# Prologue of an attention kernel by input tile and token half, maxima by query tile, queries one group ahead

## The reference

```python
sa, ca, ga, sb, cb, gb = silu(c) @ wmod            # six rows of 512, from one row c of 512
h = layernorm(x) * (1 + ca) + sa
q = rmsnorm(h @ wq_a.T) @ wq_b.T                   # 128 wide, then 32 heads of 64 + 64
ckv, k_pe = split(h @ wkv_a.T, [32, 64])
k_nope, v = split(rmsnorm(ckv) @ wkv_b.T, [64, 128])   # for each of 32 heads
q_pe, k_pe = rope(q_pe), rope(k_pe)
attn = softmax(causal(q_full @ k_full.T * scale))
x = x + floor(ga) * ((attn @ v) @ wo.T)
h = layernorm(x) * (1 + cb) + sb
x = x + floor(gb) * ffn(h)                         # silu(gate) * up, down, width 1376
```

## Time and profile before

| what | us |
|---|---|
| median of 3 runs (lowest, highest) | 862.09 (860.8, 863.05) |
| the profiled execution, its time | 862.18 |
| its span, first to last instruction | 860.4 |
| busy: PE, PEld | 785.7, 531.4 |
| busy: DVE, ACT, POOL | 533.1, 271.5, 327.7 |
| first scores of the eight groups | 140.49, 202.09, 262.66, 324.03, 384.58, 445.05, 505.65, 560.01 |
| last values of the eighth group, end of its last record | 610.16 |
| mean granted clock of PE (1 is full speed) | 0.958 |

### The profile page before, as it was taken

One profiled execution on the slowest core, in us unless ns is written; L12 is line 12 of the kernel. 1 busy time (PEld: TensorE's weight loads), 2 busy tenths in 40 slices (PEclk: granted clock), 3 DMA queues, 4 the chain that ended last, 5 costly groups with the idle time before them and its releaser, 6 DMA issues.

```text
span 860.4 us, 10667 instructions
## 1 busy us (share of the span) xinstructions
PE 785.7 (91%) x3968; PEld 531.4 (62%) x3968; DVE 533.1 (62%) x836; ACT 271.5 (32%) x402; POOL 327.7 (38%) x199
## 2 busy tenths in 40 slices
PE   5659597999998999999999999999799899999997
PEld 5658254564664655656656655544487688886886
DVE  3354484896896896987978977756465333222342
ACT  2360002333433433433343333343344332221220
POOL 9220022374574574484564663524344100000111
PEclk9895687999999999999999999999899899999999
DMA  8300714306107007016034057046000032220011
GB/s 343 114 0 1 158 52 98 64 1 131 32 0 161 2 2 161 1 32 132 1 70 93 1 106 262 2 147 220 1 1 0 1 111 74 73 65 1 24 38 37
DMA packets 30275, 60.49 MB, mean 70 GB/s; under 512 B 4656, under 2 KB 16688, under 8 KB 28432
## 3 DMA queue, kind: packets, MB, share of 16 engines
q1 hardware_dynamic: 29024, 57.11, 24.8%
q10 hardware_dynamic: 1200, 2.69, 0.8%
HBM read 32.40 MB, written 2.10 MB: 40 GB/s over the span
## 4 chain that ended last, share of the span: by engine, by line
PE 60%; issue 12%; DVE 8%; POOL 7%; SPq 4%; DMA 4%; ACT 3%; POOLq 0%; ACTq 0%; DVEq 0%
PE PS L691 14%; PE PS L585 7%; PE PS L530 6%; PE PS L662 5%; PE PS L588 5%; PE PS L586 5%; PE PS L601 4%; POOL PR L1389 3%; DMA Q<-TQ 3%; SPq L386 2%; PE PS L459 2%; PE PS L521 2%; PE PS L534 1%; POOL RE L1354 1%; PE PS L512 1%
## 5 line engine op out<-in xcount | busy, mean ns | idle before, releaser
L817 ACT ACTIVATE PR<-PS 128x1024 f32<-128x1024 f32 (+1 forms) x144 | 132.9, 929 | 262.1 <-PE PS L588 183.5
L1085 DVE TENSOR_REDUCE NMa<-PS 128x1 f32<-128x512 f32 (+3 forms) x216 | 140.3, 665 | 44.4 <-PE PS L534 29.0
L530 PE MATMUL PS<-KH,Q 96*128 96x512 f32 (+3 forms) x384 | 132.2, 400 | 12.7 <-DMA Q<-TQ 10.6
L585 PE MATMUL PS<-Q,KH 128*128 128x512 f32 x288 | 132.5, 460 | 3.7 <-DMA Q<-NM 2.6
L1389 POOL TENSOR_TENSOR PR<-PR 128x1024 f32<-128x1024 f32 (+3 forms) x56 | 119.8, 2139 | 27.9 <-ACT PR L817 24.1
L691 PE MATMUL PS<-Q 128*128 128x512 f32 (+1 forms) x528 | 123.2, 396 | 5.1 <-DVE Q L1253 4.5
L691 PEld LDWEIGHTS PS<-Q 128*128 128x128 f32 (+1 forms) x528 | 99.3, 189 | 28.1 <-DVE Q L1253 4.7
L588 PE MATMUL PS<-Q,KH 128*128 128x512 f32 x288 | 114.6, 398 | 0.0
L586 PE MATMUL PS<-Q,KL 128*128 128x512 f32 x288 | 114.3, 397 | 0.0
L530 PEld LDWEIGHTS PS<-KH,Q 96*128 96x128 f32 x384 | 71.9, 196 | 49.2 <-issue 20.1
L585 PEld LDWEIGHTS PS<-Q,KH 128*128 128x128 f32 x288 | 56.1, 195 | 60.1 <-issue 28.2
(11 more groups left out here) (161 smaller groups left out, 1084.4 us busy)
## 6 DMA issues: line engine op xcount, KB each, us to landing
Q<-TQ SPq DMA_DIRECT2D x96, 256.0 KB, 5.0
PR<-in_wmod SPq DMA_DIRECT2D x6, 1024.0 KB, 7.2
RT<-in_wo SPq DMA_DIRECT2D x4, 1024.0 KB, 4.9
TQ<-in_wo SPq DMA_DIRECT2D x4, 1024.0 KB, 4.9
WI<-in_gate_w SPq DMA_DIRECT2D x10, 256.0 KB, 3.2
WI<-in_up_w SPq DMA_DIRECT2D x10, 256.0 KB, 3.6
DI<-in_down_w SPq DMA_DIRECT2D x10, 256.0 KB, 3.6
TQ<-in_x ACTq DMA_DIRECT2D x2, 1024.0 KB, 10.3
```

The lines of the kernel that those rows point to most:

```text
L530: ins = pe.matmul(bank[:, i * w:(i + 1) * w], M.Q[0:KR, g % 2, 0, h0 + i, qt * P:(qt + 1) * P], M.KH[0:KR, lo:lo + w], start=(i == 0), sto ...
L585: pe.matmul(dst, M.KH[:, ks], M.Q[:, w % 2, 0, :, qs], start=True, stop=False)
L817: act.activation(tiles, banks, ACT.Exp).then_inc(S_.p, 1)
L1085: dve.tensor_reduce(dst, PS[:, bank_of(turn), 0:n * w].rearrange("p (h k) -> p h k", k=w), axis=AX.X, op=ALU.max, negate=True).then_inc(S_ ...
```

## The change

**Prologue.** The inputs arrive by tile, into a place of their own. Moments, root and reciprocal are taken by tile: those of tiles 0 to 2 ahead, the later ones inside the tile loop, three tiles ahead. hH and hL have four places each in place of two. The rotated key parts and the copy to V move from VectorE to GpSimd (`keys`), the two roots of a tile become one. The latents use one PSUM bank in place of two. Group 0's weight folds stand in the loop after tile 3, the queries of the first 512 tokens after tile 7, those of the second half behind the loop. Only group 0's queries are made in the prologue. The columns n = 2 and 3 of the modulation and the two gate rows move into the windows of groups 0 and 1, and their tables are loaded later and to other places. The zeros in rows 96 to 127 of KH, KL and Q go, and the score products read 97 or 96 rows.

**Maxima.** `PARTS` is sorted by token half first: 11 parts for query tiles 0 to 3, then 27 for tiles 4 to 7. Each half has its own 16 columns, transposition and transfer. The transposition of the first half of group w + 1 stands at the end of window w, that of the second half behind the values of step 1 of window w + 1; the scores wait for the first at step 0 and for the second at step 4. In the prologue only the first half of group 0 is made.

**Queries.** The window of group w holds the queries of group w + 1, at places 0.03 to 0.30, and its maxima from 0.36 on, which run over into window w + 1. A half is sent as four transfers of 384 KB, one for each head, as soon as it is ready. An add counts in the table with 560 columns a microsecond in place of 850.

```diff
-    return sorted(parts, key=lambda part: part[3] + part[4])
+    return sorted(parts, key=lambda part: (part[0] >= NS // 2, part[3] + part[4]))
 
 
 PARTS = maxima_parts()
+FIRST = sum(part[0] < NS // 2 for part in PARTS)
...
-        self.Q = take("Q", [P, 2, 2, HG, S], F32R)
+        self.Q = take("Q", [P, 2, 2, NQB, HG, QB], F32R)
-        self.NMa = take("NMa", [P, HG, NS])
+        self.NMa = take("NMa", [P, 2, HG, NS // 2])
-        self.NM = take("NM", [HG * NS, P], F32R)
+        self.NM = take("NM", [HG * NS // 2, 2, P], F32R)
-        self.hH = take("hH", [P, 2, KD, P], F32R)
-        self.hL = take("hL", [P, 2, KD, P], F32R)
+        self.x = take("x_in", [P, NS, D])
+        self.hH = take("hH", [P, 4, KD, P], F32R)
+        self.hL = take("hL", [P, 4, KD, P], F32R)
...
+        self.wmod = [self.PR[:, 0], self.PR[:, 1], late_mod[2], late_mod[0], late_mod[0], late_mod[1]]
...
-QUERY_PLACES = [(0.13, ("w", 0), 0.5), (0.14, ("w", 1), 0.15), (0.15, ("w", 2), 0.15), (0.25, ("even", 0), 1.2),
-                (0.28, ("odd", 0), 1.2), (0.36, ("lat", 0), 1.3), (0.40, ("split", 0), 0.0),
-                (0.54, ("even", 1), 1.2), (0.57, ("odd", 1), 1.2), (0.65, ("lat", 1), 1.3), (0.75, ("split", 1), 0.0)]
-WINDOW_US = 56.0
+QUERY_PLACES = [(0.03, ("w", 0), 0.5), (0.035, ("w", 1), 0.15), (0.04, ("w", 2), 0.15), (0.06, ("even", 0), 1.2),
+                (0.09, ("odd", 0), 1.2), (0.13, ("lat", 0), 1.3), (0.16, ("split", 0), 0.0),
+                (0.20, ("even", 1), 1.2), (0.23, ("odd", 1), 1.2), (0.27, ("lat", 1), 1.3), (0.30, ("split", 1), 0.0)]
+WINDOW_US = 60.0
...
+def maxima_places(parts, begin, end):
+
+    cost = [0.14 + PARTS[k][2] * PARTS[k][4] / 960 for k in parts]
     places = []
+    for n, k in enumerate(parts):
+        places.append((begin + (end - begin) * sum(cost[:n]) / sum(cost), ("part", k), cost[n]))
+        if k == FIRST - 1:
+            places.append((places[-1][0] + 0.015, ("rows", 0), 0.3))
+    return places + [(end + 0.01, ("join",), 0.1), (end + 0.02, ("rows", 1), 0.3)]
+
+
+
+FIRST_HALF = [[("part", w, k) for k in range(FIRST)] + [("rows", w, 0)] for w in range(G)] + [[]]
+SECOND_HALF = [[("part", w, k) for k in range(FIRST, len(PARTS))] + [("join", w), ("rows", w, 1)] for w in range(G)]
...
+    if w < G - 1:
+        coming = maxima_places(range(len(PARTS)), 0.36, 1.16)
+        places += [(place, (name[0], w + 1) + name[1:], busy) for place, name, busy in coming]
+        places += [(place, (name[0], w + 1) + name[1:], busy) for place, name, busy in QUERY_PLACES]
+    if w == 0:
+        rest = maxima_places(range(FIRST, len(PARTS)), 0.0, 0.22)
+        places += [(place, (name[0], w) + name[1:], busy) for place, name, busy in rest]
+        places += [(0.45, ("modrow", w, 0), 0.7), (0.60, ("modrow", w, 1), 0.7), (0.75, ("mod", w, 2), 0.2)]
+    else:
+                places += [(0.09, ("den", w - 1, 1), 0.7), (0.10, ("inv", w - 1, 1), 0.8), (0.17, ("norm", w - 1, 1), 0.0)]
+    if w == 1:
...
+            due = {("v", 1): SECOND_HALF[w], "last": FIRST_HALF[w + 1]}.get(spot, [])
+            while places and (any(name in due for _, name, _ in places) or max(places[0][0], free - SLACK) <= place):
...
+FIRST_FOLDS = [("w", 0, i) for i in range(3)]
+FIRST_QUERIES = [[(kind, 0, hf) for kind in ("even", "odd", "lat", "split")] for hf in range(2)]
+FIRST_MAXIMA = [("part", 0, k) for k in range(FIRST)] + [("rows", 0, 0)]
+BANKED = ("w", "even", "odd", "lat", "part", "rows", "den", "fold", "mod", "modrow")
...
-    def send_queries(g):
-        sp.wait_ge(S_.tl, 2 * (g + 1))
+    def send_queries(g, hf):
+        cols = slice(hf * 512, hf * 512 + 512)
+        sp.wait_ge(S_.tl, 2 * g + hf + 1)
         if g > 1:
             sp.wait_ge(S_.sc, NEXP * (g - 1))
         for h in range(HG):
-            for b in range(3):
-                sp.dma_start(M.Q[b * 32:(b + 1) * 32, g % 2, :, h, :].bitcast(F32),
-                             M.TQ[h * 32:(h + 1) * 32, b, :, :].bitcast(F32)).then_inc(S_.q[h], 16)
-
-    def send_maxima(g):
-        sp.wait_ge(S_.free, TURN[("rows", g)] + 1)
-        sp.dma_start(M.Q[KR:KR + 1, g % 2, 0, :, :].rearrange("p h (n q) -> p (h n) q", q=P).bitcast(F32),
-                     M.NM[:].bitcast(F32)).then_inc(S_.nd, 16)
+            sp.dma_start(M.Q[0:KR, g % 2, :, hf, h, :].bitcast(F32),
+                         M.TQ[h * L:(h + 1) * L, :, :, cols].bitcast(F32)).then_inc(S_.q[hf][h], 16)
+
+    def send_maxima(g, hf):
+        sp.wait_ge(S_.free, TURN[("rows", g, hf)] + 1)
+        sp.dma_start(M.Q[KR:KR + 1, g % 2, 0, hf].rearrange("p h (n q) -> p (h n) q", q=P).bitcast(F32),
+                     M.NM[:, hf, :].bitcast(F32)).then_inc(S_.nd, 16)
...
+    load_weights(0)
     sp.dma_start(M.cos[:], t["cos"]).then_inc(S_.tables, 16)
     sp.dma_start(M.sin[:], t["sin"]).then_inc(S_.tables, 16)
-    load_weights(0)
-    sp.wait_ge(S_.pads, 7)
-    send_queries(0)
     load_weights(1)
-    load_mod(5)
-    send_maxima(0)
+    for hf in range(2):
+        send_queries(0, hf)
+    send_maxima(0, 0)
+    sp.wait_ge(S_.ql, NS)
+    for n in (4, 5, 2):
+        load_mod(n)
     for w in range(G - 1):
         if w < G - 2:
             load_weights(w + 2)
-        send_queries(w + 1)
+        send_maxima(w, 1)
+        send_queries(w + 1, 0)
+        send_queries(w + 1, 1)
+        if w == 0:
+            sp.wait_ge(S_.side, TURN[("modrow", 0, 0)] + 1)
+            load_mod(3)
...
+        send_maxima(w + 1, 0)
+    send_maxima(G - 1, 1)
...
-    def maxima_rows(g):
-        bank = side_bank(TURN[("rows", g)])
-        pe.wait_ge(S_.nm, g + 1)
-        pe.transpose(bank[0:HG * NS, 0:P], M.NMa[:].rearrange("p h n -> p (h n)"), M.ident[:]).then_inc(S_.side, 1)
+    def maxima_rows(g, hf):
+        bank = side_bank(TURN[("rows", g, hf)])
+        if hf == 0:
+            pe.wait_ge(S_.free, TURN[("part", g, FIRST - 1)] + 1)
+        else:
+            pe.wait_ge(S_.nm, g + 1)
+        pe.transpose(bank[0:HG * NS // 2, 0:P], M.NMa[:, hf].rearrange("p h n -> p (h n)"), M.ident[:]).then_inc(S_.side, 1)
...
-        if s == 0 and i == 0:
-            pe.wait_ge(S_.nd, 16 * (w + 1))
+        if kt == 0 and i == 0:
+            pe.wait_ge(S_.nd, 16 * (2 * w + qb + 1))
...
-        pe.matmul(dst, M.KH[:, ks], M.Q[:, w % 2, 0, :, qs], start=True, stop=False)
-        pe.matmul(dst, M.KL[:, ks], M.Q[:, w % 2, 0, :, qs], start=False, stop=False)
+        pe.matmul(dst, M.KH[0:KR + 1, ks], M.Q[0:KR + 1, w % 2, 0, qb, :, qs], start=True, stop=False)
+        pe.matmul(dst, M.KL[0:KR, ks], M.Q[0:KR, w % 2, 0, qb, :, qs], start=False, stop=False)
...
             project_inputs(st - 1)
         if 0 <= st - 3 < NS:
             turn_latents(st - 3)
-
+        if st == 3:
+            for key in FIRST_FOLDS:
+                side(key)
+        if st == NS - 1:
+            for key in FIRST_QUERIES[0]:
+                side(key)
     pe.wait_ge(S_.mask, 4)
-    pe.wait_ge(S_.pads, 7)
-    pe.wait_ge(S_.ql, NS)
-    pe.wait_ge(S_.scb, 1)
-    columns = [(n, d) for n in (2, 3) for d in range(KD)]
-    for _, name, _ in QUERY_PLACES:
-        side((name[0], 0) + name[1:])
-        if len(columns) > 4:
...
+    def root(st):
+        act.wait_ge(S_.mv, 2 * st + 2)
+        act.activation(M.rstd[:, st:st + 1], M.mv[:, st, 1:2], ACT.Sqrt, bias=M.eps[:, 1:2]).then_inc(S_.sq, 1)
...
-        act.activation(M.rms[:, b, 0:1], M.ms[:, b, 0:1], ACT.Sqrt, scale=1.0 / R, bias=M.eps[:, 0:1]).then_inc(S_.rt, 1)
-        act.activation(M.rms[:, b, 1:2], M.ms[:, b, 1:2], ACT.Sqrt, scale=1.0 / L, bias=M.eps[:, 0:1]).then_inc(S_.rt, 1)
+        act.activation(M.rms[:, b, :], M.ms[:, b, :], ACT.Sqrt, bias=M.eps[:, 0:1]).then_inc(S_.rt, 1)
...
+    for st in range(NS + 3):
+        if st + 3 < NS:
+            root(st + 3)
+        if st < NS:
+            modulate(st)
+        if 0 <= st - 2 < NS:
+            roots(st - 2)
+        if 0 <= st - 3 < NS:
+            latents_high(st - 3)
+        if st == 3:
...
+    for st in range(NS + 3):
+        if st + 3 < NS:
+            moments(st + 3)
+        if st + 1 < NS:
+            normalise(st + 1)
+        if 0 <= st - 2 < NS:
+            scale(st - 2)
+        if st < NS:
+            h_high(st)
+        if 0 <= st - 3 < NS:
+            latents_low(st - 3)
...
+    def keys(st):
+        b = st % 2
+        rot = M.rot[:, b].rearrange("p r (c n) -> p r c n", c=2)
+        pool.wait_ge(S_.cr, st + 1)
+        pool.tensor_copy(M.V[:, st, :], M.key_parts(b)[:, 2])
+        pool.tensor_tensor(M.key_parts(b)[:, 0:2], rot[:, 0], rot[:, 1], ALU.add).then_inc(S_.kr, 1)
```

452 lines of the change are left out of this document (208 added, 244 removed).

## The result

The changed kernel takes 939.75 us (931.66 to 940.74, 4 runs) where the kernel before takes 861.82 (860.80 to 863.05, 4 runs): 1.088 times as long, interval 1.082 to 1.095. The profiled execution takes 939.47, with a span of 937.7, against 862.18 and 860.4. The prediction of 861.1 with a range to 873 missed it by 78.

What follows compares the result with a forecast made beforehand. TensorE was taken to bound the groups, chains the prologue. From 862.2 us, -46.7 for the prologue, +25.6 for work moved into the groups and +20.0 for new waits gave 861.1, range 846 to 873.

Steps and rivals of the forecast that it cites:

- The prologue: Before the first scores: they start at 93.8 (bounds 90 to 97), a change of -46.7 us.
- Rival 3: Prologue doesn't pipeline: each of eight tiles takes 1 us more, scores start at 103, total 870; chance 0.08.
- The gate rows: Moved into the groups: eight pairs of records at 0.46 each, 3.7 us of TensorE work.
- The added transpositions: In the groups: one more transposition of maxima per group at 0.2 us, 1.6 in all.
- The join's wait: At the second half's transposition, groups 2 to 6: TensorE waits 2.1 to 3.0 us, taken as 2.6.
- the join's 0.25: At a group's head: VectorE's join of maxima costs 0.25 us within a chain of 3.2 to 4.2.
- The rule of exclusion: At a group's head: VectorE's add might wait out GpSimd's 2.75 us split, adding up to 10 us in all.
- The wait for the transfer: At step 4: TensorE waits 1.3 to 1.7 us for the second half's maxima to be sent, taken as 1.5.
- rival 1: Clock falls at the new waits at group heads: 871 in four of seven groups, up to 880 in all; chance 0.20.
- the column products: Two later ones moved into groups 0 and 1: 64 records cost 6.9 us at the high clock, at most 9.5.
- the edit to 97 and 96 rows: Score products in the groups: fewer rows in place of 128 cost nothing either way.
- Today's 1.14 at each transposition never did it: Argument against the clock falling at new waits: existing 1.14 us waits at each transposition had not lowered it.

Runs made afterwards that it cites:

- e5: The changed kernel with its two late column products cut into four pieces of four products each, spread over windows 0 and 1; 935.0 us.
- e1: The kernel before with one edit: score products read 97, 96 and 96 rows in place of 128; 863.2 us, ratio 1.003.
- e8: e4 with column products in four pieces and maxima ended earlier, at 0.88 of window 0 and 0.76 of the others; 866.1 us, ratio 1.0045.
- e9: e8 with score products of 128 rows and the maxima ended at 0.74 in windows 1 to 6; 867.7 us.
- e3: The changed kernel with the split of the first half's queries moved behind the join and the transposition; 947.7 us.
- e4: The changed kernel with queries two groups ahead and all maxima inside the window before, except group 0's second half; prologue kept; 895.8 us.
- e11: The changed kernel with queries two groups ahead and column products spread, the second half of the maxima still in its own span; 921.0 us.
- e14: e3 with score products of 128 rows; 924.3 us.
- e12: e5 with score products of 128 rows; 908.8 us.
- e13: e11 with score products of 128 rows; 884.6 us.
- e6: The changed kernel with score products of 128 rows again, the rows past 96 being zeros written by GpSimd; 906.6 us.

## Why the prediction was wrong

**What bounds: right.** PE's work in a group is what it was, and everything put there cost its length.

**The prologue: right, a little too dear.** First scores at 89.08, forecast 93.8 (90 to 97). PE's timeline of the changed kernel:

```profile
54.62 0.79 PE L515 MATMUL PS<-WAH,hH 128*128 128x288 f32 x4 [2.68 <-POOL hL L1369]
...
66.73 0.47 PE L524 MATMUL PS<-ident,qn 128*128 128x128 f32 x1 [6.16 <-POOL key L1376]
...
89.08 0.79 PE L621 MATMUL PS<-Q,KH 97*128 97x512 f32 x1 [2.19 <-DMA Q<-NM]
```

The seventh tile's projection stands at 54.6, forecast 58.3: the rounds overlapped more than the sum of steps allows. Everything behind it ran as worked out, 4 to 5 earlier, the wait of 6.16 for the last two tiles' keys behind the queries among it. Rival 3 is refuted.

**Work moved in: right in sum.** 27.2 against 25.6, but two terms were wrong and partly offset each other. The gate rows were put at 3.7, with 0.46 read as the length of a pair of records; 16 records run, and eight of them take 3.7:

```profile
147.06 3.70 PE L493 MATMUL PS<-wide 128*128 128x512 f32 x8 [0.69 <-DVE NMa L1094]
```

The added transpositions, put at 1.6, do not show: a middle group's work is 58.5 before and after.

**Waits: right in kind, half in size.** 37.2 against 20.0. The join's wait was put at 2.1 to 3.0 and is 3.5: the step that failed is the join's 0.25, which the prediction took from a place where GpSimd was ending its split (VectorE's and GpSimd's rows of the kernel before):

```profile
258.75 0.23 DVE L1090 TENSOR_TENSOR NMa<-NMa,NMb 128x16 f32<-128x16 f32 x1
...
255.87 3.08 POOL L1360 TENSOR_TENSOR TQ<-RE,TQ 128x1024 fp32r<-128x1024 f32 x1 [0.93 <-ACT TQ L791]
```

The rule of exclusion was in the text, but applied to the add alone. The wait for the transfer was put at 1.5 and is 0.4. What was missing altogether are 1.5 at the first half's transposition and 1.3 at the denominators in each middle group. Group 7 waits 3.9 more than before where 1.5 was forecast, 2.8 of it for a load of the output weights.

**The clock: the term that failed.** The forecast gave it nothing, and rival 1, at 0.20, gave it at most 19. It was 65. The rival's mechanism and place were right for the falls behind the join's wait, but three steps of its sizing were wrong. It priced one low stretch of 6.8 for each group; the middle groups have 10 to 17, and groups 0 and 1 have 25 and 44. It looked only at the new waits, while the clock also fell at 346.40, after 0.5 of waits, and in or behind the column products: their row, within which the clock fell, was read as a price for PE's time alone (what they cost inside a group is open, e5). And the edit to 97 and 96 rows was costed at nothing, for the reason that such products follow each other at the same pace. So they do (e1); what they change is how often the clock falls in groups that wait 5 to 9 us, 23 to 36 us here. "Today's 1.14 at each transposition never did it" was a fact about groups with 128-row products that wait some 2 us in all.

The Trainium skill (TensorE: Matmul & The Clock Gate, "HAM oscillation") tells of a loop that waits for data and starts each round at the low clock. The low stretches behind the join's wait of 3.5 are this form, once in each of groups 2 to 6. But this trace also has a fall behind 3.50 us of unbroken work, and 23.9 us at the low clock without a wait, which that section does not lead one to expect; here the measurement decides.

**What stays open.** Why some low stretches last 20 us and more with PE busy throughout, and others 3.4, was not settled: 128 rows did not shorten the one of 24 from the prologue into group 0 (e8 to e9). Nor was it shown what the column products cost: the clock fell in or behind their blocks, but cutting them up gained only with narrow score products. Nor was the prologue tried alone, without the second set of queries in group 0.

## What to carry to other kernels

Price TensorE's waits at more than their length, and read the granted clock's column before trusting a sum of busy times: here 7.2 us of waits in a group cost 4.9 more through the clock, and a group that did 7 us of useless work in its waits was faster than one that waited. What TensorE does between waits counts too: score products of 96 rows cost more at the same waits than those of 128. When two engines hold each other out, moving one operation away can move the exclusion to the next (e3); an earlier place for the step that is waited for, with the other engine idle beside it, took the wait away (e4 to e8).

## What the runs showed of the hardware

- Score products of 97 and 96 rows in place of 128 take the same time (58.6 of PE work in a group against 58.5), but in group 3, with waits of 4.7 to 9.3, its mean clock is lower: 0.88 to 0.93 against 0.95 to 0.97 (e3, e5, e11 and the changed kernel against e14, e12, e13 and e6).
- 32 records of one-column products, 3.63 us with PE busy all the time, were followed by 23.9 us at 0.50. A stretch of 20.5 at 0.50 stood in group 0 of the same kernel without them.
- With 97 and 96 rows the clock fell at 346.40 of the changed kernel after 0.5 us of waits in 7.9 us.
- VectorE's join of 16 columns took 0.16 to 0.18 alone, 1.59 to 1.82 beside GpSimd's split in the changed kernel and 1.23 to 2.31 beside GpSimd in e4, ending 0.03 to 0.04 behind GpSimd's operation each time.
